# Sheaf layer: 90 of 125 edge columns summed in PSUM, comparisons placed between the scans

## The reference, cut to what matters

```python
def reflection(a, b):
    return relu(concatenate([a, b], axis=1) @ W1.T + b1) @ W2.T + b2
F_s = householder(reflection(xs, xd))          # xs = x[src], xd = x[dst]
F_d = householder(reflection(xd, xs))
L_sd = -einsum('eki,ekj->eij', F_s, F_d)
msg_s = coef[:, None] * einsum('eij,ej->ei', L_sd, xd)
msg_d = coef[:, None] * einsum('eji,ej->ei', L_sd, xs)
out = x - zeros_like(x).at[src].add(msg_s) - zeros_like(x).at[dst].add(msg_d)
return relu(out)
```

## Time and profile before

| | us |
|---|---|
| median of 3 runs (lowest, highest) | 23112.76 (23050.33, 23122.42) |
| the profiled execution | 23039.02 |
| its span, first to last instruction | 23037.1 |
| sheaf chunks 1 to 24, from wait to wait | 8154.6 to 14252.3 |

### The profile page before, as it was taken

How to read it: one execution, slowest core, us unless ns; L and a number is a source line. 1 busy time by engine, 2 the same in 40 slices (tenths; PEclk the granted TensorE clock), 3 DMA queues, 4 the chain that set the end, 5 groups by cost and what they waited for, 6 DMA issues and landing times. The chain is left out here.

```text
span 23037.1 us, 291747 instructions
## 1 busy us (share of the span) xinstructions
PE 18150.1 (79%) x98910; PEld 13788.4 (60%) x98910; DVE 13778.7 (60%) x24271; ACT 6244.1 (27%) x8041; POOL 16691.9 (72%) x14269
## 2 busy tenths in 40 slices
PE   0688882699997178888878888389999988999997
PEld 0344442344443167777777777389999986555556
DVE  2788883455554155555555555367777772777772
ACT  0000000000000066777766777311111111111111
POOL 5777774777776588888888887487777751777775
PEclk9888885799998588888888888689999998999998
DMA  2122220111111112111111111122222221888884
GB/s 98 45 61 61 61 62 23 38 42 47 42 43 40 17 30 39 29 29 29 29 31 37 29 29 26 32 52 44 42 41 46 42 32 61 251 252 249 251 252 123
DMA packets 1853618, 1604.27 MB, mean 70 GB/s; under 512 B 671719, under 2 KB 1624198, under 8 KB 1835094
## 3 DMA queue, kind: packets, MB, share of 16 engines
q0 software_dynamic: 781216, 459.51, 13.0%
q10 hardware_dynamic: 821300, 579.22, 8.1%
q1 hardware_dynamic: 249730, 548.09, 7.1%
HBM read 906.08 MB, written 679.64 MB: 69 GB/s over the span
## 5 line engine op out<-in xcount | busy, mean ns | idle before, releaser
L802 POOL DMA_INDIRECT gathered<-gat_table,src_index x4810 | 4829.6, 1004 | 1496.1 <-issue 1471.1
L1444 POOL DMA_INDIRECT acc<-column_sums,sum_rows x2625 | 4815.0, 1834 | 1288.6 <-issue 779.6
L1385 PE MATMUL node_sums<-placed_row,lane_values 128*128 128x392 f32 x22200 | 4480.8, 353 | 7.3 <-DVE placed_row L1343 3.8
L1684 POOL DMA_INDIRECT gathered<-sheaf_table,src_index x3125 | 3554.9, 1138 | 963.3 <-issue 957.4
L1385 PEld LDWEIGHTS node_sums<-placed_row,lane_values 128*128 128x128 f32 x22200 | 3977.7, 190 | 190.2 <-issue 157.9
L2479 POOL DMA_INDIRECT gathered<-message_table,src_index x2381 | 2363.0, 992 | 727.4 <-issue 725.1
L1009 PE MATMUL lanes_ps<-S,table_parts 128*128 128x512 bf16 x9828 | 2266.9, 393 | 334.3 <-DVE S L874 334.3
L1009 PE MATMUL lanes_ps<-code_onehot,table_parts 128*128 128x512 bf16 x9828 | 2217.4, 387 | 156.1 <-DVE code_onehot L874 156.1
L1343 DVE TENSOR_SCALAR placed_row<-iota_rows_f,src_row 128x1568 fp32r<-128x1568 f16 x1500 | 1570.5, 1055 | 848.9 <-PE node_sums L1385 843.7
L1358 ACT ACTIVATE row_distance<-iota_rows_f,src_row 128x1568 bf16<-128x1568 f16 x1275 | 2035.5, 1596 | 25.7 <-issue 10.0
L1009 PEld LDWEIGHTS lanes_ps<-S,table_parts 128*128 128x128 bf16 x9828 | 983.9, 101 | 1554.1 <-DVE S L874 320.3
(11 more groups left out here) (493 smaller groups left out, 26778.9 us busy)
## 6 DMA issues: line engine op xcount, KB each, us to landing
message_rows<-gathered ACTq DMA_DIRECT2D x250, 1600.0 KB, 10.6
src_rows<-src_rows SPq DMA_DIRECT2D x150, 640.0 KB
src_rows<-src_rows SPq DMA_DIRECT2D x100, 960.0 KB
code_rows<-src_code_rows SPq DMA_DIRECT2D x360, 256.0 KB, 3.2
gat_rows<-scanned ACTq DMA_DIRECT2D x25, 3375.0 KB
gathered<-gat_table,src_index POOLq DMA_INDIRECT x4810
gat_rows<-scanned ACTq DMA_DIRECT2D x25, 2125.0 KB
start_values<-starts SPq DMA_DIRECT2D x50, 1062.5 KB, 5.1
```

Source lines behind the costliest of these rows:

```text
L802: g.indirect_dma_start(G[b][:, j, :], None, tab, bass.IndirectOffsetOnAxis(ap=IX[b][:, j:j + 1], axis=0)).then_inc(s_g[b], 16)
L1385: last = pe.matmul(o.acc[:, m, 0:Q8 // 4], lane, o.OW[r][:, m * (Q8 // 4):(m + 1) * (Q8 // 4)], start=first(k, 1) and i == 0 and part == 0 ...
L1444: g.indirect_dma_start(self.acc[i], bass.IndirectOffsetOnAxis(ap=o.IXS[b][:, j:j + 1], axis=0), o.SV[b][:, j, :], None, compute_op=ALU.add ...
L1684: g.indirect_dma_start(G[b][:, j, :], None, self.tab17, bass.IndirectOffsetOnAxis(ap=IX[b][:, j:j + 1], axis=0)).then_inc(s_g[b], 16)
```

## The change

1. `MT` becomes 90. Each chunk sends 35 columns to the accumulators in HBM in place of 40 (7 rounds of five, with 18 gathers ahead of each), and 90 tiles through PSUM. The number of comparisons stays 13 groups, since `EQC` doesn't depend on `MT`.
2. `GAP` becomes 15. The five added tiles stand behind the loop: 65 in the loop, 15 behind it, 10 at the end.
3. A fifth buffer of lane values, laid over `sidx`; the kept target rows shrink to 16 bits to make room, and the message layer reads 65 columns of them in place of 125.
4. DVE's order behind the loop: the one-hots are spread between the reflections; the first two comparisons stand ahead of the values, two more between the values and the scans, eight between pairs of scans, the last behind them. The top part of the split is written over `src_dst` in place of `vectors`.

```diff
-MT = 85
+MT = 90
...
-            LANES, RING, STEPS = 4, 5, 4 * SG
+            LANES, RING, STEPS = 5, 5, 4 * SG
...
+            self.sums16 = nc.alloc_sbuf_tensor_at("sum_rows_kept", [P, EP], I16, offset=self.sidx_at)
+            o.SVH.append(nc.alloc_sbuf_tensor_at("lane_values_over_index", [P, 2, ACCS, 8, D], R32, offset=self.sidx_at + 2 * EP + 22))
+            o.lanes = LANES
...
-            GAP, END = 10, 10
+            GAP, END = 15, 10
...
                         w(v.tensor_tensor(pair(Q[:]), pair(VV), spread(TT), ALU.mult))
-
-                        onehots(range(made, LOOP + GAP))
+                        onehots(LOOP + RING + 2)
                         w(v.tensor_tensor(XX, XX, Q[:], ALU.add))
+                        onehots(LOOP + RING + 4)
...
-                        onehots(range(LOOP + GAP, LOOP + GAP + RING))
+                        for g in range(o.nq):
+                            self.equal(v, o, k, b, g)
                         v.tensor_copy(VAL[:, :, D:DW], bcast(self.order_w[:].unsqueeze(1), [P, EQC, 3]))
...
                         v.sem_inc(s_val, 1)
+                        onehots(LOOP + GAP + RING)
                         w(v.tensor_tensor(VP, Q[:, SC:CH, 0:D], bcast(DP[:, SC:CH].unsqueeze(2), [P, MT, D]), ALU.mult))
+                        self.equal(v, o, k, b, o.nq)
                         self.lanes(v, w, o)
+                        self.equal(v, o, k, b, o.nq + 1)
...
                         for f in range(D):
                             ins = v.tensor_tensor_scan(OUT[b][:, :, f], sm, Q[:, :, D + f], OUT[1 - b][:, CH - 1, f:f + 1], ALU.mult, ALU.add)
+                            if f % 2 and g < o.sums:
+                                self.equal(v, o, k, b, g)
+                                g += 1
...
-                        for g in range(o.sums):
-                            self.equal(v, o, k, b, g)
+                        for i in range(g, o.sums):
+                            self.equal(v, o, k, b, i)
...
-                        w(v.tensor_copy(self.sidx[:, ds(k * CH, EQC)], o.IXS[b][:, 0:EQC]))
+                        w(v.tensor_copy(self.sums16[:, ds(k * CH, EQC)], o.IXS[b][:, 0:EQC]))
...
-                        v.tensor_copy(o.IXS[b][:], self.sidx[:, ds(k * CH, CH)]).then_inc(o.s_ixs, 1)
+                        v.tensor_copy(o.IXS[b][:, 0:EQC], self.sums16[:, ds(k * CH, EQC)]).then_inc(o.s_ixs, 1)
```

More of the change, by code:

```diff
@@ L21 @@
 I32 = mybir.dt.int32
+I16 = mybir.dt.int16
 BF16 = mybir.dt.bfloat16
@@ L1600, in sheaf_edges @@
             flat = Q[:].rearrange("p c f -> p (c f)")
-            LANES, RING, STEPS = 4, 5, 4 * SG
+            LANES, RING, STEPS = 5, 5, 4 * SG
             parked = [nc.alloc_sbuf_tensor_at(f"placed_over_features{i}", [P, Q8], R32, offset=self.x_at + 4 * Q8 * i)[:] for i in range(2)]
-            self.tile_buffers(c, o, MT, parked + [sb(f"placed_row{i}", [P, Q8], R32)[:] for i in range(RING - len(parked))], LANES,
+            self.tile_buffers(c, o, MT, parked + [sb(f"placed_row{i}", [P, Q8], R32)[:] for i in range(RING - len(parked))], LANES - 1,
                               V[:].rearrange("p c f -> p (c f)")[:, 0:Q8], 2, R32)
+            self.sums16 = nc.alloc_sbuf_tensor_at("sum_rows_kept", [P, EP], I16, offset=self.sidx_at)
+            o.SVH.append(nc.alloc_sbuf_tensor_at("lane_values_over_index", [P, 2, ACCS, 8, D], R32, offset=self.sidx_at + 2 * EP + 22))
+            o.lanes = LANES
+            assert (2 * EP + 22) % 32 == 0 and 2 * EP + 22 + 2 * ACCS * 8 * D * 4 <= 4 * EP
             o.IO16 = sb("iota_rows_f16", [P, Q8], F16)
@@ L1623, in sheaf_edges @@
             FST, o.IXF = (CNTB[:, (3 + i) * EQC:(4 + i) * EQC] for i in range(2))
-            top_at = EQC * DW + MT * D
-            assert top_at + MT * D <= CP * 2 * D
-            top = V[:].rearrange("p c f -> p (c f)")[:, top_at:top_at + MT * D].rearrange("p (c f) -> p c f", f=D)
+            assert EQC * DW + MT * D <= CP * 2 * D and MT * D <= CH * 2 * D
+            top = XY[:].rearrange("p c f -> p (c f)")[:, 0:MT * D].rearrange("p (c f) -> p c f", f=D)
             srcc = sb("src_chunk", [P, CH])
@@ L1845, in open_lanes, with onehots @@
                                     self.lane_values(v, o, k - 1, 1 - b, t, wide)
-                        def onehots(r):
+                        made = [0]
+                        def onehots(upto):
                             if not first(k, 1):
-                                for i in r:
+                                for i in range(made[0], upto):
                                     self.mixed_dve(v, o, k - 1, 1 - b, i)
-                        onehots(range(0, RING))
+                            made[0] = upto
+                        onehots(RING)
                         open_lanes(0, 2)
-                        made = RING
                         pair = lambda ap: ap.rearrange("p c (a f) -> p c a f", a=2)
@@ L1856, in compute @@
                             open_lanes(opened[q - 1] if q else 2, opened[q])
-                            upto = at_step[min(4 * q + 4, STEPS - 1)].stop + RING
-                            onehots(range(made, upto))
-                            made = upto
+                            onehots(at_step[min(4 * q + 4, STEPS - 1)].stop + RING)
                             if q == 0 and not first(k, 1):
@@ L1918, in compute @@
                         w(v.tensor_tensor(o.IXS[b][:, 0:EQC], FST, srcc[:, 0:EQC], ALU.add))
-                        w(v.tensor_copy(self.sidx[:, ds(k * CH, EQC)], o.IXS[b][:, 0:EQC]))
+                        w(v.tensor_copy(self.sums16[:, ds(k * CH, EQC)], o.IXS[b][:, 0:EQC]))
                         v.sem_inc(o.s_ixs, 1)
-                        onehots(range(LOOP + GAP + RING, MT))
+                        onehots(MT)
                         if first(k, 1):
```

7 lines of the change are left out of this document (6 added, 1 removed).

## The result

The changed kernel takes 22910.76 us (median of four runs, 22856.29 to 22930.46), the kernel before in the same series 23098.04 us. The ratio is 0.9918 with a 95% interval of 0.9894 to 0.9942: 187 us less, where 180 were forecast, and the time lies 22 us under the forecast of 22933. The profiled execution took 22856.29 us with a span of 22853.6, 183.5 less than before.

The account below looks back on a forecast made before the run. POOL (265.5 us a chunk) was taken to bound the kernel, the DVE-PE chain (262.3) close inside. 23 intervals give -182 us, chunk 24 -7.2, last tiles +9.8: -180, median 22933 us, range 22820 to 23015.

Parts of the forecast that it names:

- Two limits, both of which had to move: Sheaf chunks: POOL at 265.5 us and the chain through DVE and PE at 262.3; a change must move both.
- POOL, 8.3 us less a chunk: Sheaf chunks: five scatters fewer give 9.3 us, DVE's added instructions cost 1.0; ends 5.7 and 10.5.
- the second rival: Sheaf chunks: the scatters' whole mean comes free, POOL 255.0 and chain 255.1 us, 227 less, 22886; chance 18%.
- The sign named for it: POOL's DMAs: a scatter's mean rising from 1.80 and the gather's from 1.148 us would show that the delays stayed.
- The tiles behind the loop: PE behind the loop: fifteen tiles take between 22 and 34 us, inside the 33 us PE stands still.
- the ring: Behind the loop: one-hots and tiles wait for each other across two engines, 15 tiles outlast the values; 23315 us, 5%.
- The sums 9.0 us earlier, 1.6 lost to starving: DVE and PE behind the loop: earlier comparisons start the sums 9.0 us sooner, PE loses 1.6, sums end 7.4 earlier.
- The first rival: Chain: it doesn't shorten, as DVE starves PE or comparison rows come late; -55 us, 23058; chance 10%.
- Clock and pause: PE ahead of the sums: pause some 10 us in place of 33, granted clock there still 0.50.
- The last chunk: Chunk 24 gains the chain's 7.2 us; five more tiles of the last chunk, standing alone, cost 9.8.
- Sum: Whole kernel: 23 intervals fall from 265.1 to 257.2 us, -182; with chunk 24 and last tiles, -180 together.

Follow-up runs that it names:

- e1: Changed kernel with MT = 85 and GAP = 10 again, keeping DVE's new order and the fifth lane buffer; 23105.43 us, ratio 1.0007 to the kernel before.
- e2: Changed kernel with all 13 comparisons behind the scans again, keeping 90 columns in PSUM; 23095.92 us, ratio 1.0005 to the kernel before.
- e4: Changed kernel with only 115 of 125 source columns gathered; interval 255.47 us, 22877.73 us in one run.
- e4b: Kernel before the change with only 115 of 125 source columns gathered; interval 262.54 us, 23041.14 us in one run.
- e5: Changed kernel with five scatters more a chunk, DVE untouched; interval 267.29 us, 23134.31 us in one run.
- e9: Changed kernel unaltered, timed again in another series; 22906.40 us, ratio 0.9931 to the kernel before.
- e6: e5 with DVE's 128x4000 add replaced by a product with one operand in PSUM; interval 262.73 us, 23024.78 us in one run.

## Why the prediction was right, point by point

- **Two limits, both of which had to move.** Right. e1 and e2 move one each and give 1.0007 and 1.0005; e4 and e4b show the inner one by itself.
- **POOL, 8.3 us less a chunk.** 7.74 in the interval, a little less. Three terms make it up. Five scatters are worth 9.9 us (9.3 taken). The five tiles' added instructions cost 267.29 - 266.68 = 0.6 (e5 against e1; 1.0 taken). The new order costs 266.68 - 265.12 = 1.6 by itself, which the prediction put at nothing; the delays of 165 DMAs show most of it, 37.1 us in e1 for 35.7 before. So the terms were off by 0.6 and 0.4 to the one side and 1.6 to the other, and that they nearly cancel is luck. That the delays stay with DVE's instructions, the choice of 8.3 between the ends 5.7 and 10.5, held; the second rival with 255.0 us for POOL did not. The sign named for it, both means rising, came out by half: the gather's fell, since the DMA beside the add is a scatter now.
- **The tiles behind the loop.** 33 us, inside the 22 to 34; they end 9.4 us ahead of the sums, and the ring did cost PE pauses of 2 us each without deciding.
- **The sums 9.0 us earlier, 1.6 lost to starving.** From the first lane values behind the loop to the sums it was 52.7 us and is 44.1: 8.6 earlier. The sums last 1.4 us longer, with the late fifth comparison where it was expected. Net 7.2 for 7.4; the chain 6.9 for 7.2. The first rival needed comparisons that starve PE throughout, and from the seventh on DVE waits.
- **Clock and pause.** The pause of 33 us became 9.44 (10 forecast), and the clock stayed at 0.50.
- **The last chunk.** Chunk 24 with the tiles behind it, -7.2 + 9.8 = 2.6 forecast, 3.0 measured.
- **Sum.** The intervals gave 178.0 of the 182 forecast. (The sum took POOL's 257.2 from the mean interval of 265.1 and not from POOL's own 265.5, so it counted 7.9 of the 8.3 us.) The profiled pair then came to -183.5 with the help of 13.9 us from ahead of the sheaf layer, which no edit touches. Without them it is 169.6, and the second series (e9) gave 165: the closeness of 187 to 180 is partly luck.

## What to carry to other kernels

Work out each limit of a loop by itself: POOL's program as instructions times their durations, the chain as the interval minus its wait. Where two lie as close as here (265.1 and 262.3 us), an edit that moves one can be worth nothing alone and the pair much; think of the other half before giving one up. And where VectorE is busy beside it, price a GpSimd DMA at its undelayed duration first (9.3 us for five scatters, 9.9 measured): the rest of its mean went here with what VectorE does beside it.

## What the runs showed of the hardware that was not expected

- An add of two SBUF tensors costs POOL 4.6 us more in a chunk than a product of the same length with an operand in PSUM (e5, e6); cut in four it delays less (3.6 to 2.5 us by overlap).
- DVE can pause about 5.2 us in each turn of a loop, released by nothing in the trace, and 20 or 60 memsets ahead of the loop, executed once, end it (3723.7 to 3682.1 and 3680.6 us). Two kernels that differ far ahead of a loop can so differ in it.
- The first wait for a gather in the sheaf layer ended anywhere from 7964.7 to 8043.0 us in the profiled executions, with the code of the attention layer ahead the same in all; the sheaf intervals of one kernel agreed within 0.1 us. Small gains are read from the stage, not from one total.
